# Choosing the two best experts in the attention iterations in place of the scan stage

## The reference

```python
def _gate(x, Wsel):
    s = jax.nn.sigmoid(jnp.einsum('bsd,hed->bhse', x, Wsel))
    _, idx = jax.lax.top_k(s, K)
    mask = jax.nn.one_hot(idx, E, dtype=s.dtype).sum(-2)
    return s * mask

def _moe_attn(x, Wq, Wk, Wv, Wo, Wsel_v, Wsel_o):
    q = _rope(jnp.einsum('bsd,hdp->bhsp', x, Wq))
    k = _rope(jnp.einsum('bsd,hdp->bhsp', x, Wk))
    gv = _gate(x, Wsel_v)
    v = jnp.einsum('bsd,bhse,hedp->bhsp', x, gv, Wv)
    att = jax.nn.softmax(jnp.einsum('bhsp,bhtp->bhst', q, k) / np.sqrt(P), axis=-1)
    o = jnp.einsum('bhst,bhtp->bhsp', att, v)
    go = _gate(x, Wsel_o)
    return jnp.einsum('bhsp,bhse,hepd->bsd', o, go, Wo)
```

## Time and profile before

| | us |
|---|---|
| median of 3 runs | 4552.34 (4547.19 to 4552.66) |
| profiled execution | 4550.93 |
| its span, first to last instruction | 4549.1 |
| TensorE busy | 3873.6 (85%) |
| VectorE busy | 3483.8 (77%) |
| GpSimd busy | 2705.4 (59%) |
| ScalarE busy | 2037.9 (45%) |

### The profile page before, as it was taken

How to read it: one execution, slowest core, us unless ns; L and a number is a source line. 1 busy time by engine, 2 the same in 40 slices (tenths; PEclk the granted TensorE clock), 3 DMA queues, 4 the chain that set the end, 5 groups by cost and what they waited for, 6 DMA issues and landing times. The chain is left out here.

```text
span 4549.1 us, 52321 instructions
## 1 busy us (share of the span) xinstructions
PE 3873.6 (85%) x16256; PEld 2698.3 (59%) x16256; DVE 3483.8 (77%) x3612; ACT 2037.9 (45%) x3761; POOL 2705.4 (59%) x1772
## 2 busy tenths in 40 slices
PE   6776766857666399999999999999999999999787
PEld 2232322323222277777777777777777777777676
DVE  5999999999999566666666666666666666666598
ACT  4544534435343144444444444444544544444443
POOL 2756656566476365665665666656655755665454
PEclk7786777868776699999999999999999999999899
DMA  1000000000000210010010000000100100000001
GB/s 37 0 10 14 10 19 19 9 14 9 23 9 10 76 62 14 14 39 9 14 39 9 32 21 14 35 14 14 39 9 14 39 9 14 19 14 9 34 28 42
DMA packets 48726, 97.83 MB, mean 22 GB/s; under 512 B 3570, under 2 KB 33138, under 8 KB 46228
## 3 DMA queue, kind: packets, MB, share of 16 engines
q1 hardware_dynamic: 47620, 92.94, 5.8%
q0 software_dynamic: 1040, 4.19, 0.2%
HBM read 80.34 MB, written 16.78 MB: 21 GB/s over the span
## 5 line engine op out<-in xcount | busy, mean ns | idle before, releaser
L723 DVE TENSOR_TENSOR_SCAN state<-dA,dBx 128x2048 f32<-128x2048 f32 x128 | 706.5, 5519 | 9.3 <-POOL y_part L309 4.3
L1015 POOL TENSOR_TENSOR qk_full<-vg 128x512 f32<-128x512 f32 x256 | 329.9, 1289 | 455.6 <-DVE vg L1330 455.6
L1230 ACT ACTIVATE prob<-ps_b,negmax 128x512 f32<-128x512 f32 x512 | 346.1, 687 | 549.3 <-DVE negmax L1336 549.3
L306 POOL TENSOR_TENSOR state<-state,c_copy 128x1024 f32<-128x1024 f32 x120 | 302.0, 2516 | 420.6 <-DVE state L723 420.6
L396 PE MATMUL ps_a<-xp_high,ident_r 33*128 33x512 f32 x256 | 163.3, 638 | 425.1 <-DVE dBx L713 399.7
L1330 DVE TENSOR_TENSOR vg<-ps_b,gates 128x1024 f32<-128x1024 f32 x256 | 313.6, 1225 | 255.0 <-PE ps_b L1072 251.2
L573 ACT ACTIVATE dA<-dt,a_neg 128x511 f32<-128x511 f32 x512 | 326.9, 711 | 398.3 <-DVE state L723 397.9
L1029 POOL TENSOR_TENSOR ogT_low<-prob,ogT_high 128x512 fp32r<-128x512 f32 x256 | 322.0, 1287 | 201.6 <-ACT ogT_high L1261 201.6
L1070 PE MATMUL ps_b<-wv_high,xT_high 128*128 128x512 f32 x1024 | 414.2, 404 | 0.0
L1070 PE MATMUL ps_b<-ogT_high,wo_high 128*128 128x512 f32 x1024 | 408.4, 399 | 0.0
L396 PEld LDWEIGHTS ps_a<-xp_high,ident_r 33*128 33x128 f32 x256 | 59.5, 232 | 583.2 <-DVE dBx L713 488.6
(11 more groups left out here) (232 smaller groups left out, 9658.0 us busy)
## 6 DMA issues: line engine op xcount, KB each, us to landing
xT<-xT_scratch SPq DMA_DIRECT2D x65, 512.0 KB, 3.2
wv<-in_wv SPq DMA_DIRECT2D x8, 1024.0 KB, 4.9
wo<-in_wo SPq DMA_DIRECT2D x8, 1024.0 KB, 6.9
x_in<-in_x SPq DMA_DIRECT2D x8, 512.0 KB, 4.6
x_a<-in_x SPq DMA_DIRECT2D x8, 512.0 KB, 5.3
x_scratch<-x_a SPq DMA_DIRECT2D x8, 512.0 KB, 2.9
xT_scratch<-x2T SPq DMA_DIRECT2D x8, 512.0 KB, 2.6
gates_scratch<-gate SPq DMA_DIRECT2D x8, 512.0 KB, 3.5
```

Of the source, the lines that this page charges most:

```text
L723: dve.tensor_tensor_scan(h[n % 2][:, :, :].rearrange("p c s -> p (c s)"), dA[n % 2][:, :, :].rearrange("p c s -> p (c s)"), dBx[n % 2][:, ...
L1015: pool.tensor_tensor(v4[:, at, :, :], vg[:, at, 0:4, :], vg[:, at, 4:8, :], ALU.add).then_inc(vsum_done, 1)
L1230: act.activation(prob[h][:, t, :], ps[:, score_bank(t) + h, :], ACT.Exp, bias=negmax[:, t, h:h + 1], accum_out=total[:, h, t:t + 1]).then_ ...
```

## The change

The choice leaves stage A: the first lines of the diff are from the lists of GpSimd and VectorE there, all the others from the list of VectorE in stage B. Its scores are written by the sigmoids in the order of pairs (a rearranged write), and SP stores them in place of the gates, so it waits for sg_done there. In stage B the scores of a pair are loaded, and each iteration chooses for the next one, on 128 values per partition (4 tiles of 32): twelve operations, all on VectorE, the ranking product with first among them, in three places of the iteration, and a thirteenth, `keep_gates`, behind `turn_raw`. The same steps for the first iteration stand in `start`. The load of the next pair's scores is issued behind the last `keep_gates` of the pair; the first load, and one of first, stand ahead of the first weights.

```diff
             def turn(i, par, has_tail, has_head):
...
-                    if n in (11, 13) and has_tail:
-                        rank_picked(i - 1, 3 * (n - 11))
...
-                        elif n == 11:
-                            best_of(c, sg[:, :], 0)
-                        elif n == 12:
-                            first_of(c, sg[:, :], 0)
-                        elif n == 13:
-                            best_of(c, left[:, :], 6)
-                        elif n == 14:
-                            first_of(c, left[:, :], 6)
-                        elif n == 15:
-                            gates(c)
...
+            def best_of(it, k, src):
+
+                step = CREDIT + it * TOP + k
+                dve.wait_ge(top_step, step)
+                dve.tensor_reduce(top[:, :], src, AX.X, ALU.max).then_inc(top_step, 1)
+                dve.wait_ge(top_step, step + 1)
+                dve.tensor_tensor(pick[:, :, :], src, top_e, ALU.is_equal).then_inc(top_step, 1)
+                dve.wait_ge(top_step, step + 2)
+                dve.tensor_tensor(rank[:, :, :], pick[:, :, :], first_g, ALU.mult).then_inc(top_step, 1)
+
+            def first_of(it, k, src):
+
+                step = CREDIT + it * TOP + k
+                dve.wait_ge(top_step, step + 3)
+                dve.tensor_reduce(top[:, :], rank[:, :, :], AX.X, ALU.max).then_inc(top_step, 1)
+                dve.wait_ge(top_step, step + 4)
+                dve.tensor_tensor(pick[:, :, :], rank[:, :, :], top_e, ALU.is_equal).then_inc(top_step, 1)
+                dve.wait_ge(top_step, step + 5)
+                dve.scalar_tensor_tensor(left[:, :, :], pick[:, :, :], -2.0, src, ALU.mult, ALU.add).then_inc(top_step, 1)
+
+            def keep_gates(it, b):
+                dve.wait_ge(top_step, CREDIT + it * TOP + TOP)
+                dve.scalar_tensor_tensor(grouped(gates[:, :, :]), left[:, :, :], 0.0, sc(b), ALU.is_lt, ALU.mult).then_inc(gates_done, 1)
...
                 maxima(it, 0)
                 maxima(it, 1)
+                if coming:
+                    dve.wait_ge(scores_loaded, (j if more else j + 1) * 16 + 32)
+                    best_of(it + 1, 0, sc(ahead))
+                    first_of(it + 1, 0, sc(ahead))
                 gate_values(it, j, b, 1)
+                if coming:
+                    best_of(it + 1, 6, left[:, :, :])
                 maxima(it, 2)
                 maxima(it, 3)
                 gate_values(it, j, b, 2)
+                if coming:
+                    first_of(it + 1, 6, left[:, :, :])
                 gate_values(it, j, b, 3)
```

More of the change, by code:

```diff
@@ L168, in stage_a @@
         x2T = sb("x2T", [P, KD, S])
[L169 to L183, removed]
+        sg = sb("sg", [P, PAIRS, TT, GP])
         ln_x, ln_m, ln_a = (Norm(ctx, nc, n, eps[:, 0:1]) for n in ("ln_x", "ln_m", "ln_a"))
         early_tiles = dict(ident=ident, w_in=w_in, conv_w=conv_w, conv_b=conv_b)
-        const_tiles = dict(w_xp=w_xp, w_dt=w_dt, a_log=a_log, d_skip=d_skip, first=first, w_out=w_out, w_sel=w_sel)
+        const_tiles = dict(w_xp=w_xp, w_dt=w_dt, a_log=a_log, d_skip=d_skip, w_out=w_out, w_sel=w_sel)
         early_loaded, consts_loaded = sem("early_loaded"), sem("consts_loaded")
@@ L845, in _ @@
             norm_a(last)
-            best_of(last, sg[:, :], 0)
-            first_of(last, sg[:, :], 0)
-            best_of(last, left[:, :], 6)
-            first_of(last, left[:, :], 6)
-            gates(last)
 def stage_b(nc, d, const, acc):
@@ L871, in stage_b, with grouped @@
         ident = const["ident"]
-        gates = sb("gates", [P, NB * TT, GP])
+        scores_in = sb("scores", [P, NB * TT, GP])
+        gates = sb("gates", [P, TT, GP])
+        first = sb("first", [P, E])
+        GROUPS = TT * GP // E
+        top = sb("top", [P, GROUPS])
+        pick, rank, left = (sb(n, [P, GROUPS, E]) for n in ("pick", "rank", "left"))
+        def grouped(v):
+            return v.rearrange("p t (g e) -> p (t g) e", e=E)
+        top_e = top[:, :].unsqueeze(2).to_broadcast([P, GROUPS, E])
+        first_g = first[:, :].unsqueeze(1).to_broadcast([P, GROUPS, E])
         shapes = dict(wqk=[P, KD, 2, P], wv=[P, 2, KD, E * HP], wo=[P, 2, EP, D])
@@ L920, in stage_b @@
         GATE = 3
+        TOP = 12
         RAW, OUT = 0, 6
@@ L957, in pair, with load_scores @@
                     load_xT(b + 1)
+                if more:
+                    sp.wait_ge(gates_done, j * NB + NB)
+                    load_scores(j + 1)
                 sp.wait_ge(xT_low, CREDIT + j * NB + NB)
                 load_xT(0)
+            def load_scores(j):
+                sp.dma_start(scores_in[:, :, :].unsqueeze(1), d["scores"][bass.ds(j, 1)].rearrange("j p b t c -> p j (b t) c")).then_inc(scores_loaded, 16)
             sp.dma_start(vg[:, 0:2, :, :].rearrange("p t e n -> p (t e n)"), d["spread"]).then_inc(consts_loaded, 16)
             load_xT(0)
+            sp.dma_start(first[:, :], d["first"]).then_inc(scores_loaded, 16)
+            load_scores(0)
             load_weights(0)
@@ L1382, in batch @@
             def batch(it, j, b, more, more_pairs):
+                coming, ahead = more or more_pairs, b + 1 if more else 0
                 gate_values(it, j, b, 0)
@@ L1401, in batch @@
                     turn_raw(it + 1)
+                    keep_gates(it + 1, ahead)
                 for e in range(EP):
@@ L1788, in program @@
     d["x1"] = nc.dram_tensor("x1_scratch", (NB, S, D), F32, kind="Internal").ap()
-    d["gates"] = nc.dram_tensor("gates_scratch", (PAIRS, P, NB, TT, GP), F32, kind="Internal").ap()
+    d["scores"] = nc.dram_tensor("scores_scratch", (PAIRS, P, NB, TT, GP), F32, kind="Internal").ap()
     with nc.sbuf_tensor("ident", [P, P], F32) as ident:
```

76 lines of the change are left out of this document (28 added, 48 removed).

## The result

The changed kernel takes 4641.3 us (median of 4 runs, 4632.3 to 4645.4) against 4552.5 us: a ratio of 1.0194, with a 95% interval from 1.0176 to 1.0212. It is slower by 89 us, where 172 were forecast. The profiled execution took 4632.28 us, its span 4630.5, which is 81 us more than the span before.

The account below looks back on a forecast made before the run. VectorE was taken to bound stage A, TensorE the attention stage. 4550.9 - 107 (stage A) + 214 (blocking) + 63 (clock) + 3 (start) = 4724 us; range 4540 to 4830.

Parts of the forecast that it names:

- Stage A, 107 us forecast: Time stage A gives back without the choice: 77 in six turns, 11 in the seventh, 19 after the last.
- the first turn has a head and no tail: Stage A's first turn makes no choice, so its 77.60 us stretch measures six later turns without it: 77 us saved.
- the seventh turn: Last stretch in stage A, gives less than the mean of 12.9 because GpSimd's last y_part is needed: 11 us.
- the tail: After stage A's last turn nothing covers the choice, from first maximum to store: 18.9 us saved.
- Blocking in the attention stage, 214 us: GpSimd blocks added VectorE steps between maxima and probabilities, making probT_low 3.4 us late in 63 iterations.
- The clock, 63 us: TensorE's longer waits in the attention stage partly lower its clock, 1.0 us per iteration.
- with two gaps of some 2 us each the attention stage resembles the last stage: TensorE, about 41 of 45 us busy per attention iteration, would near the last stage's granted clock of 0.95.
- Start, 3 us: Start of the attention stage: thirteen operations fit VectorE's 21.2 us idle time, but loads and blocking cost 0 to 6.
- Nothing gives it back: After the late attention product all engines shift alike to the iteration's end, so the whole 3.4 us remains.
- Rival (b): Attention stage: blocking as worked out, but TensorE's clock stays at 2.4 GHz; 4661 us, chance 29%.
- the places of the two waits: Sign: TensorE waits 1.5 us at the first transposes and 2 us at the first product with probT.
- Rival (a): Attention stage: no blocking by such short operations, only the chain's own length costs, 57 us; 4504 us, chance 16%.

Follow-up runs that it names:

- r1_reductions: Changed kernel with each of the twelve choice steps replaced by a one-input maximum of a fixed 128-element tile, same places and chain; 4449.0 us.
- r10_before: The kernel before, unchanged, profiled once more; 4549.8 us, ratio 0.9998.
- r2_none: Changed kernel with the twelve choice steps left out of the attention stage and the start, only the thirteenth operation kept; 4433.4 us.
- r6_gap: Changed kernel with six further 128-element reductions ahead of the first probT_low; 4841.3 us.
- r4_g2_early: Changed kernel with only the second group of three steps moved, directly behind the first six; 4609.9 us.
- r1_scalars: Changed kernel with the eight two-input choice steps replaced by products of one SBUF tensor with a constant, the four reductions kept; 4611.8 us.
- r7_start: r3_moved with VectorE's wait for the cosine and sine tables moved to just ahead of turn_raw, and the first loads reordered; 4439.7 us.
- r3_moved: Changed kernel with the whole second choice and the thirteenth operation moved behind low_outputs, ahead of low_qk; 4439.9 us.
- r11_keep_late: Changed kernel with only the thirteenth operation moved, from behind turn_raw to behind low_outputs; 4644.7 us.

## Why the prediction came out as it did

The direction and the mechanism were right, the sizes less so: 173 us were added up and 81 measured between the spans. The price is made by the blocking of short steps, not by VectorE's load. `r1_reductions` shows it: same places, same chain, 2.57 us less per iteration. By term:

- **Stage A, 107 us forecast.** 132 measured (the span up to the memset that opens the attention stage, 1574.2 before and 1442.3 after). The step that failed is "the first turn has a head and no tail": that yardstick of 77.60 us was itself one unlucky execution. Over six turns its 3 us are 18, and those stretches gave 96 us (543.0 to 447.1) where 77 were forecast. The other terms: 2 in the rest of the six turns, 11 in the seventh turn (as forecast), 20 in the tail (forecast 19), and 3 in the first turn itself, by the same chance. The prediction named "much more than 107 us" itself as a sign of being wrong. With both lengths taken from `r10_before` the same sum for the six turns gives 92 us (539.8 less 6 x 74.65).
- **Blocking in the attention stage, 214 us.** In a plain iteration probT_low is 2.83 us late (forecast 3.4): the third maximum starts 7.63 us after the first (forecast 7.99), since the ranking product was issued a tenth of a microsecond behind GpSimd's 0.74 and ended with it, where the forecast let a whole 0.73 pass and then added its own time; the other 0.2 us are between there and the fourth product. 0.1 is given back at the next maximum. 48 plain iterations x 2.72 = 131 us. The 14 iterations at changes of pair, which the prediction didn't look at, cost 5.2 each, 73 us in all. Of these 5.2, 0.8 stay without any choice (`r2_none`) and 1.3 are the clock of the next term; the other 3.1 are near the 2.7 of a plain iteration. Together 204, of which 19 are the clock: 185 against the 214.
- **The clock, 63 us.** Mis-sized: 38 us at half clock, 19 us lost, all at the changes of pair, and none in plain iterations. The step "with two gaps of some 2 us each the attention stage resembles the last stage" failed: they were 0.96 and 1.87 us. At 3.7 us, in `r6_gap`, every iteration has its fall; but `r4_g2_early` and `r1_scalars` have falls in plain iterations with no wait above 1.9 us, so the length of the waits isn't all of it.
- **Start, 3 us.** 7 up to the first output gate, 4.1 of them the chain. The 21 us of idle time of the earlier trace rows couldn't be used, since the chain stood behind the wait for the tables. Nor would they have been a cover: `r7_start` uses them and gains 0.7 us, for the reason that the prediction had given, GpSimd's splitting of the weights.
- "Nothing gives it back" held but for the 0.1, and keep_gates did get in ahead of the rotation in plain iterations (0.27 us as its median), but not at the changes.
- Rival (b), 4661, with blocking and no loss of clock, is nearest to what happened; the forecast erred high on the blocking (29 us) and on the clock (44), and low on what stage A gives (25), all to the same side. Of its signs, the comparisons, the reductions and the places of the two waits came true; the stretches of stage A (73.1 to 75.2 us, not 76 to 79) and the granted clock (0.99, not 0.94 to 0.98) did not. Rival (a) was wrong on the changed kernel, and `r1_reductions` runs at 4449, below its 4504.

## What to carry to other kernels

Here a short elementwise VectorE operation in SBUF cost what GpSimd had in hand at that moment (up to 2.3 us), not its own 0.29 us. So place such a step by GpSimd's list, directly ahead of something that waits for that same GpSimd result anyway, and not by VectorE's idle time. The move out of the scan stage was worth 111 us here with the second choice in such a place (`r3_moved`, 2.5% faster), and cost 89 us in the places chosen. A gain of a few us in one trace says nothing of an edit until the stages ahead of it have been compared too (`r7_start`). A stretch that is to serve as a yardstick for six others should be read in more than one execution.

## What was not expected of the hardware

- A product of one tensor with a constant is blocked as a two-input one is: 1225 ns against 226 alone.
- Falls of the clock don't follow from the amount of idle time alone. With the second group moved (`r4_g2_early`), TensorE idles less than in the changed kernel (2.9 against 3.7 us per iteration by its busy time), and its clock falls 30 times against 8. In `r1_scalars` both waits are shorter than in the changed kernel (0.65 and 1.77 against 0.97 and 1.88 us), and yet all of its 8 falls lie in plain iterations. Why is open.
- In `r11_keep_late` one blocked operation was moved to where it holds up nothing; the waits went, and in the traced execution the time came back as lost clock.
- Two traces of the same kernel differ by 3 us in one stretch of 75 (77.60 and 74.65), and by 6.7 us at the end of stage A (1574.2 and 1567.5).
